# Layer-1 pairs moved from two SBUF buffers into one PSUM bank, and the other banks divided anew

## What is computed

```python
x0 = xk = e                                   # (1024, 39, 16)
for W in (f0, f1, f2):                        # (39*39, 128), (128*39, 128), (128*39, 128)
    z = einsum('bfd,bgd->bfgd', x0, xk).reshape(b, 39 * g, 16)
    cur = einsum('bpd,pm->bmd', z, W)         # (1024, 128, 16)
    outs.append(cur); xk = cur
z = concatenate(outs, axis=1).sum(-1)         # (1024, 384)
h = relu(concatenate([z, dense_ctx]) @ W_top1 + b_top1)
h = relu(h @ W_top2 + b_top2)
y = h @ W_top3                                # (1024, 1)
```

## Time and profile before

| | us |
|---|---|
| median of 3 runs | 1325.23 (1324.9 to 1326.23) |
| the profiled execution | 1326.9, with a span of 1325.1 |
| PE busy in the span | 1274.4 (96%) |
| DVE, POOL, ACT busy | 1157.1 (87%), 1052.0 (79%), 913.7 (69%) |

### The profile page before, as it was taken

The page is one execution under the profiler, slowest core; times in us unless marked ns, Lnnn a source line. Parts: engine busy times, 40 slices in busy tenths (PEclk is TensorE's granted clock), DMA queues, the critical chain, the costliest instruction groups (busy, mean ns, idle before and its releaser), DMA issues. The chain is left out here.

```text
span 1325.1 us, 21626 instructions
## 1 busy us (share of the span) xinstructions
PE 1274.4 (96%) x5983; PEld 1015.7 (77%) x5983; DVE 1157.1 (87%) x3210; ACT 913.7 (69%) x3053; POOL 1052.0 (79%) x743
## 2 busy tenths in 40 slices
PE   3899999999999999999999999999999999999998
PEld 2587777877788777887778877788777877788787
DVE  3599998799988999689996999969998799988983
ACT  2477776677767777577775777757776677767783
POOL 7688888688877888778986888968888688874661
PEclk9799999999999999999999999999999999999999
DMA  5582233332223332213333033331233332223000
GB/s 135 104 206 46 49 62 65 62 62 43 43 52 63 63 65 58 43 34 62 67 64 64 5 64 66 65 61 23 51 62 65 62 58 44 46 54 61 1 3 1
DMA packets 129499, 76.33 MB, mean 58 GB/s; under 512 B 90792, under 2 KB 98201, under 8 KB 129379
## 3 DMA queue, kind: packets, MB, share of 16 engines
q1 hardware_dynamic: 119139, 72.32, 26.8%
q0 software_dynamic: 10240, 2.64, 2.3%
HBM read 68.42 MB, written 3.87 MB: 55 GB/s over the span
## 5 line engine op out<-in xcount | busy, mean ns | idle before, releaser
L397 ACT ACTIVATE parts<-pieces,x_cols 128x128 f32<-128x128 f32 x2560 | 716.0, 376 | 172.3 <-PE pieces L693 156.3
L531 DVE SCALAR_TENSOR_TENSOR parts<-pieces,x_cols,parts 128x128 f32<-128x128 f32 x2432 | 679.9, 341 | 115.5 <-PE pieces L693 89.6
L691 PE MATMUL pieces<-w_hi,cur_hi 128*128 128x512 f32 (+1 forms) x1280 | 548.3, 428 | 18.2 <-DVE parts L531 16.8
L693 PE MATMUL pieces<-w_hi,cur_lo 128*128 128x512 f32 (+1 forms) x1280 | 498.9, 390 | 0.0
L692 PE MATMUL pieces<-w_lo,cur_hi 128*128 128x512 f32 (+1 forms) x1280 | 498.5, 389 | 0.0
L346 POOL TENSOR_TENSOR parts<-parts 128x1024 f32<-128x1024 f32 x127 | 320.1, 2520 | 134.8 <-DVE parts L531 131.4
L337 POOL DMA_INDIRECT emb<-in_table,rows x320 | 345.1, 1078 | 80.9 <-issue 67.4
L691 PEld LDWEIGHTS pieces<-w_hi,cur_hi 128*128 128x128 f32 x1280 | 241.8, 189 | 89.4 <-DVE parts L531 38.4
L693 PEld LDWEIGHTS pieces<-w_hi,cur_lo 128*128 128x128 f32 x1280 | 240.9, 188 | 51.6
L692 PEld LDWEIGHTS pieces<-w_lo,cur_hi 128*128 128x128 f32 x1280 | 242.2, 189 | 47.8
L416 ACT ACTIVATE pairs_hi<-pairs 117x512 fp32r<-117x512 f32 (+1 forms) x224 | 141.9, 634 | 193.8 <-DVE pairs L541 161.9
(11 more groups left out here) (69 smaller groups left out, 594.7 us busy)
## 6 DMA issues: line engine op xcount, KB each, us to landing
partners<-x_wide SPq DMA_DIRECT2D x62, 546.0 KB
partners<-x_wide SPq DMA_DIRECT2D x31, 468.0 KB
x_rep<-x_wide SPq DMA_DIRECT2D x96, 78.0 KB
emb<-in_table,rows POOLq DMA_INDIRECT x320
x_diag<-x_cols SPq DMA_DIRECT2D x256, 10.0 KB
x_wide<-emb SPq DMA_DIRECT2D x32, 80.0 KB
x_wide<-emb SPq DMA_DIRECT2D x32, 32.0 KB
wt<-in_wt SPq DMA_DIRECT2D x1, 1024.0 KB
```

The costliest lines, as they stand in the source:

```text
L397: last = nc.scalar.activation(parts[n % 2][:, 4 * i + r, :], src[:, r * H:(r + 1) * H], ACT.Copy, scale=x_cols[n // 4][:, n % 4, f:f + 1])
L531: nc.vector.scalar_tensor_tensor(acc, src[:, r * H:(r + 1) * H], x_cols[n // 4][:, n % 4, f:f + 1], acc, ALU.mult, ALU.add).then_inc(acc_d ...
L691: nc.tensor.matmul(dst[:, 0:width], hi[:, cols], w1_hi[:, ws], start=True, stop=False)
L693: nc.tensor.matmul(dst[:, 0:width], lo[:, cols], w1_hi[:, ws], start=False, stop=True).then_inc(l2d_ready if q in D_PIECES else l2a_ready, 1)
```

## The change

The eight banks are divided anew.

- `pairs` is one bank of PSUM in place of two buffers of SBUF. `make_pairs` writes it, ACT's high part and DVE's low part read it. With one buffer, `make_pairs` waits for the low part of the round before (it was: of the one two before). The first tile's pairs stay in SBUF (in `partners[0]`), so the load of tile 2's partners gets a wait for the seventh low part.
- `gx_bank` holds both the 320 columns of `make_g` and, behind them, the turned fields (39 rows turned in place of 78). So a turning waits for the copy of the last G, and `make_g` waits for the copy of the last turned fields. The turning is at s = 17 of every tile (it was 14, 20, 30 and 20).
- `cur1_bank` takes, beside the first layer's sum, layer 3 and the tower. They run between two such sums: `layer3` in ten steps of four fields at 39 to 48, its copy at 49; `top1` at 79 to 82, ReLU at 83 and 84; `top2` at 86 and 87, ReLU at 88; `top3` at 119. They wait until the sum before has been taken, and the next `sum_pairs` (s = 10, that is at 50, 90 and, in the next tile but one, 130) waits for `l3_copied`, `h2_copied` and `y_copied`.
- The first four G of a quad, which must follow layer 3, move from steps 38, 42, 52, 62 to 49, 53, 60, 64; there are three `cur2` buffers in place of two.
- The pieces keep five banks.

```diff
-XT_ROWS = 2 * F
-X_STEP = XT_ROWS
+X_AT = 320
...
-S_G = [2, 12, 22, 32]
-S_G_FIRST = [2, 12, 22, 38]
-
-L3_STEP = 3
-S_L3 = range(25, 25 + F // L3_STEP)
-S_L3_COPY = 38
-S_H1 = range(41, 41 + N1 // P)
-S_RELU1 = range(45, 47)
-S_H2 = range(50, 50 + N2 // P)
-S_RELU2 = 52
-S_Y = 55
+S_X = 17
+
+
 G_LAG = 3
+G_STEP = {10 * n + 32: (0, n) for n in range(4, BLOCKS - G_LAG)}
+G_STEP.update({49: (0, 0), 53: (0, 1), 60: (0, 2), 64: (0, 3), 2: (1, 13), 12: (1, 14), 22: (1, 15)})
+
+L3_STEP = 4
+S_L3 = range(39, 39 + (F + L3_STEP - 1) // L3_STEP)
+S_L3_COPY = 49
+S_H1 = range(79, 79 + N1 // P)
+S_RELU1 = range(83, 85)
+S_H2 = range(86, 86 + N2 // P)
+S_RELU2 = 88
+S_Y = 119
 Q_HALVE, Q_FINISH = 7, 8
+CURS = 3
...
-S_X = [14, 20, 30, 20]
...
+def g_made(u, at):
+    late = [s for s, (back, _) in G_STEP.items() if s < at and (back == 0 or u > 0)]
+    return max(0, u * BLOCKS - G_LAG) + len(late)
+
+
+def x_turned(u, at):
+    return min(QUADS * TILES, u * TILES + 1 + len([i for i in range(TILES) if 4 * PIECES * i + S_X <= at]))
...
-        pairs = [sb(f"pairs{i}", [KPART, COLS]) for i in range(2)]
...
-        xbank = bank("xbank")
+        pairs = bank("pairs")
         cur1_bank = bank("cur1_bank")
-        gbank = bank("gbank")
-
-        h_sums = [xbank[:, m * P:(m + 1) * P] for m in range(N1 // P)]
+        gx_bank = bank("gx_bank")
+
+        x_turns = [gx_bank[:, X_AT + j * F:X_AT + (j + 1) * F] for j in range(4)]
+        h_sums = [cur1_bank[:, m * P:(m + 1) * P] for m in range(N1 // P)]
         h1_last = [pieces[m][:, 0:P] for m in range(N1 // P)]
-        h2_last = [pieces[4][:, m * P:(m + 1) * P] for m in range(N2 // P)]
+        h2_last = [pairs[:, m * P:(m + 1) * P] for m in range(N2 // P)]
...
+        first_banks = pieces + [pairs, gx_bank]
+        first_pairs = partners[0]
...
+                if tile == 2:
+                    sp.wait_ge(pairs_lo_ready, PAIRK)
...
+                src = gx_bank[:, X_AT:X_AT + 4 * F].rearrange("p (j f) -> p j f", f=F)
+                nc.scalar.activation(x_cols[i][:, :, 0:F], src, ACT.Copy).then_inc(x_cols_ready, 1)
...
-                nc.scalar.activation(pairs_hi[buf][0:rows, :], pairs[buf][0:rows, :], ACT.Copy
-                                     ).then_inc(pairs_hi_ready, 1)
+                src = first_pairs[0:rows, k, :] if tile == 0 else pairs[0:rows, :]
+                nc.scalar.activation(pairs_hi[buf][0:rows, :], src, ACT.Copy).then_inc(pairs_hi_ready, 1)
...
-                wait(dve, pairs_lo_ready, g - 1)
-                nc.vector.tensor_tensor(pairs[buf][0:rows, :], partners[i % 2][0:rows, k, :], x_rep[i % 2][0:rows, :],
+                dve.wait_ge(pairs_lo_ready, g)
+                nc.vector.tensor_tensor(pairs[0:rows, :], partners[i % 2][0:rows, k, :], x_rep[i % 2][0:rows, :],
...
-                nc.vector.tensor_tensor(pairs_lo[buf][0:rows, :], pairs[buf][0:rows, :],
+                src = first_pairs[0:rows, k, :] if tile == 0 else pairs[0:rows, :]
+                nc.vector.tensor_tensor(pairs_lo[buf][0:rows, :], src,
...
+            def transpose_x(tile, i, gs):
 
                 pe.wait_ge(x_rep_loaded[i % 2], (tile - i % 2) * 8 * REP + 16 * REP)
                 wait(pe, x_cols_ready, tile)
-                if i == 2 and not first:
-                    pe.wait_ge(y_copied, (tile - i) // TILES)
+                wait(pe, g_copied, gs)
                 for j in range(4):
-                    last = nc.tensor.transpose(xbank[:, j * X_STEP:(j + 1) * X_STEP],
-                                               x_rep[i % 2][0:XT_ROWS, j * P:(j + 1) * P], ident[0:XT_ROWS, 0:XT_ROWS])
+                    last = nc.tensor.transpose(x_turns[j], x_rep[i % 2][0:F, j * P:(j + 1) * P], ident[0:F, 0:F])
...
+                if first_banks[k] is gx_bank:
+                    pe.wait_ge(x_cols_ready, 1)
...
+                    if i == 2:
+                        wait(pe, l3_copied, tile // TILES)
+                    if i == 3:
+                        wait(pe, h2_copied, tile // TILES)
+                    if i == TILES:
+                        wait(pe, y_copied, tile // TILES - 1)
...
+            def make_g(u, n, turned=QUADS * TILES):
 
                 g = u * BLOCKS + n
                 pe.wait_ge(cur2_ready, g + 1)
+                pe.wait_ge(x_cols_ready, turned)
...
-                    pe.wait_ge(x_cols_ready, tiles)
-                for f in range(step * L3_STEP, (step + 1) * L3_STEP):
-                    last = nc.tensor.matmul(xbank[:, 0:P], w2[:, f, :], G[:, :, f, :], start=f == 0, stop=f == F - 1)
-                if step == F // L3_STEP - 1:
+                    pe.wait_ge(cur1_lo_ready, tiles)
+                    pe.wait_ge(sum1_ready, tiles)
+                for f in range(step * L3_STEP, min(F, (step + 1) * L3_STEP)):
+                    last = nc.tensor.matmul(cur1_bank[:, 0:P], w2[:, f, :], G[:, :, f, :], start=f == 0, stop=f == F - 1)
+                if step == len(S_L3) - 1:
...
+            def top3(u, tiles=QUADS * TILES):
                 pe.wait_ge(h2_copied, u + 1)
+                pe.wait_ge(cur1_lo_ready, tiles)
+                pe.wait_ge(sum1_ready, tiles)
```

More of the change, by code:

```diff
@@ L127, in cin_kernel @@
         tails = [sb(f"tails{i}", [P, 4, H]) for i in range(2)]
-        cur2 = [sb(f"cur2_{i}", [P, H]) for i in range(2)]
+        cur2 = [sb(f"cur2_{i}", [P, H]) for i in range(CURS)]
         x_diag = [sb(f"x_diag{i}", [P, 4, BLK_B, FX]) for i in range(2)]
@@ L483, in quad @@
                             weigh_piece(u, n, q)
+                        at = 4 * PIECES * i + s
                         if more and s in S_HIGH:
                             take_pairs_high(tile + 1, i + 1, S_HIGH.index(s))
-                        if more and s == S_X[i] + 1:
+                        if more and s == S_X + 1:
                             copy_x_cols(tile + 1, (i + 1) % TILES)
-                        if s - 1 in (S_G_FIRST if i == 0 else S_G):
-                            if n >= G_LAG:
-                                copy_g(u, n - G_LAG)
-                            elif not first:
-                                copy_g(u - 1, BLOCKS + n - G_LAG)
-                        at = 4 * PIECES * i + s
+                        if at - 1 in G_STEP:
+                            back, b = G_STEP[at - 1]
+                            if u >= back:
+                                copy_g(u - back, b)
                         if not first:
@@ L534, in make_pairs @@
             def make_pairs(tile, i, k):
-                g, buf, rows = tile * PAIRK + k, (i * PAIRK + k) % 2, rows_of(k)
+                g, rows = tile * PAIRK + k, rows_of(k)
                 if k == 0:
@@ L548, in make_first_pairs @@
                 dve.wait_ge(first_partners, k + 1)
-                wait(dve, pairs_lo_ready, k - 1)
-                nc.vector.tensor_tensor(pairs[k % 2][0:rows, :], first_banks[k % len(first_banks)][0:rows, :],
-                                        x_rep[0][0:rows, :],
+                nc.vector.tensor_tensor(first_pairs[0:rows, k, :], first_banks[k][0:rows, :], x_rep[0][0:rows, :],
                                         ALU.mult).then_inc(pairs_ready, 1)
@@ L740, in top2 @@
                     last.then_inc(h2_ready, 1)
-            def top3(u):
+            def top3(u, tiles=QUADS * TILES):
                 pe.wait_ge(h2_copied, u + 1)
+                pe.wait_ge(cur1_lo_ready, tiles)
+                pe.wait_ge(sum1_ready, tiles)
                 for k in range(N2 // P):
-                    last = nc.tensor.matmul(xbank[0:1, 0:P], wt3[:, k:k + 1], h2[:, k, :], start=k == 0,
+                    last = nc.tensor.matmul(cur1_bank[0:1, 0:P], wt3[:, k:k + 1], h2[:, k, :], start=k == 0,
                                             stop=k == N2 // P - 1)
@@ L776, in quad @@
                         n, q = 4 * i + s // PIECES, s % PIECES
+                        at = 4 * PIECES * i + s
                         layer2_piece(u, n, q)
-                        if more and s == S_X[i]:
-                            transpose_x(tile + 1, (i + 1) % TILES, first)
+                        if more and s == S_X:
+                            transpose_x(tile + 1, (i + 1) % TILES, g_made(u, at))
                         if more and s in S_SUM:
                             sum_pairs(tile + 1, i + 1, S_SUM.index(s))
-                        if s in (S_G_FIRST if i == 0 else S_G):
-                            if n >= G_LAG:
-                                make_g(u, n - G_LAG)
-                            elif not first:
-                                make_g(u - 1, BLOCKS + n - G_LAG)
-                        at = 4 * PIECES * i + s
+                        if at in G_STEP:
+                            back, b = G_STEP[at]
+                            if u >= back:
+                                make_g(u - back, b, x_turned(u, at))
                         if not first:
@@ L814, in _ @@
             make_g(u, BLOCKS - 1)
-            for step in range(F // L3_STEP):
```

(1 more changed line is left out.)

32 lines of the change are left out of this document (13 added, 19 removed).

## The result

The changed kernel takes 1332.24 us as the median of six runs (1330.91 to 1335.05), the kernel before 1325.66 us in its six (1324.9 to 1327.19). The ratio is 1.0051, with a 95% interval from 1.0038 to 1.0065. So it is slower by 0.5%, where 1315.2 us and faster was forecast, and it lies 1.2 us above the range. Three of the six runs are at 1331 us and three at 1333.4 to 1335.05. The profiled one, 1334.33 us with a span of 1332.5, is of the upper three.

What follows compares the result with a forecast made beforehand. PE's matmuls fill most of each tile; DVE, held up by POOL's adds, makes PE wait. Terms -19.2 + 11.2 - 2 = -10.0 on 1326.9 give 1316.9; the median, 1.7 lower, is 1315.2 us, range 1298 to 1331.

Steps and rivals of the forecast that it cites:

- Low part (L558) should fall to about 683 ns: DVE's 192 wide low parts, reading pairs from PSUM, fall from 949 to about 683 ns, 1.6 us a tile.
- I take 1.2 us of the 2.1 for a light tile: Tiles without layer 3 and tower: PE regains 1.2 of 2.1 us lost to waits; ends 0.3 and 2.0.
- its DVE and POOL meet as in tile 3: Reason for counting tile 0 of quads 1 to 7 among the tiles that gain 1.2 us each.
- a sign of being wrong: The forecast would be wrong if tiles without layer 3 and tower stayed above 36.2 us.
- light tiles: Tiles without layer 3 and tower, 16 after the change: -19.2 us together, between -5 and -32.
- the relief is handed back: Rival, chance 0.10: earlier DVE meets POOL in products instead; tiles without layer 3 and tower gain 0.5 us; 1326 us.
- The new waits in tile 2: PE waits for ReLUs at top2 and the sum_pairs at 90: 2.5 us a quad, net +11.2 us over seven quads.
- The turning at 17 lies five steps ahead of the next G: Turning and G share a bank; the turning at step 17 was listed as costing nothing (three steps ahead in tile 1).
- Turning 39 rows for 78: Halves 124 short PE matmuls, busy 13.9 us in all, weight loads stay: -2 us, between 0 and -5.
- The product writing to PSUM: DVE's product (L541) writes PSUM and keeps two SBUF operands: no difference, ends 0 and +0.1 us.
- The wait for the sum at step 39: DVE finishes 0.1 us before PE needs the sum: no cost, up to 0.3 us a quad if lost.

Runs made afterwards that it cites:

- The table of four: Ratios to the kernel before: pairs in SBUF 1.0071 with the waits in tile 2, 0.9985 with both ReLU steps early; pairs in PSUM 1.0051 and 0.9916.

## Why the prediction was wrong

Its sum was -10.0 us on the profiled execution; +7.4 came. By its steps:

- **"Low part (L558) should fall to about 683 ns"**: right, 679. The PSUM operand does end the block, and the longer PSUM read of the Trainium skill, "VectorE: DVE Perf Modes", section "The TRN2 errata", does not show in it: the low part of the short round, of 78 rows, takes 675 ns from PSUM, where it had 676 from SBUF.
- **"I take 1.2 us of the 2.1 for a light tile"**: this is the step that failed, with the reason given for tile 0, that "its DVE and POOL meet as in tile 3". The runs with the pairs back in SBUF measure the term by itself: the operand is worth 2.6 us of the time in place of 19.2, and 9 us once the two waits are gone. By tile: in tile 0 it wins 0.2 us with the waits (37.79 to 37.58) and 0.1 without (37.79 to 37.66); in tile 3 0.1 and 1.16. Against the kernel before, tile 0 got 0.5 us worse, 7 x 1.7 = 12 us off the forecast, and at 37.6 us it stands above the 36.2 that the prediction had named as a sign of being wrong. Quad 0's three light tiles, which were to win 3.6 us, won nothing (110.03 us before, 110.06 after). Tile 3 won 1.8 us, 3.6 us more than forecast over six quads, and that is partly luck: the pause in tile 2, put in as a pure cost, is enough for it without the operand. The working assumed that a DVE that is earlier brings POOL's add forward and so shortens the block of the first product. It did so in tile 3 (2.44 to 1.63 us). In tile 0 the first product gained 0.3, the second lost 0.85 (1.69 to 2.54) and a third, free before, took 1.68. The rival **the relief is handed back** had the mechanism, and I gave it 0.10. The run with one operand shows what all blocks of products cost once the two waits are gone, 24 us.
- **The new waits in tile 2**: right. 2.5 us a quad was the forecast, 2.47 a quad came off with them. What the prediction didn't ask is what they do to the other term: the pause relieves DVE, so the relief of the low part buys less. It allowed for the pause in tile 2 alone and added up the tiles. The table of four shows that they aren't one.
- **"The turning at 17 lies five steps ahead of the next G"**, costed at nothing: it failed too. I looked at the G behind the turning, not at the one before it, at step 12, whose copy must leave the shared bank and stands on ACT behind the high part of a blocked product. PE waits there 11.7 us in ten places. As a cause it is worth little (the copy's move gave 0.05%), since DVE would be late one piece further on.
- **The clock**: not in the sum. A wait of 2.39 us was followed by the half clock; together they cost 3.6 us in quad 5, some 2.4 of it the clock. That is likely why three runs lie 3 us above the other three: their mean clock is 0.995 against 0.996 to 0.997. Only one of the six was profiled, so this isn't shown for the others.
- **"Turning 39 rows for 78", -2**: a second failed term, of the wrong sign. The four matmuls are busy as long as before (234 ns each, from 230), and the turning holds PE 0.69 us from start to start where it held it 0.46: +0.23 a tile, up to +7 us over 31 tiles. Why is open.
- The product writing to PSUM was costed at nothing: right. Unblocked it takes 0.69 us, from 0.68. The wait for the sum at step 39 (L734 on DVE's L579) came to 1.1 us in five places.

The terms against what they measured, in us: light tiles -19.2, measured -10.8 in tile 3, +3.5 in tile 0 and 0 in quad 0; tile 2 +11.2, measured +11.2; not foreseen: the long wait and the clock in quad 5 +3.6, tile 1 +1.4. These add up to +8.9 against the +7.4 found, as close as single windows, multiplied, come. The dearer turning stands in each of these figures, 0.23 us a tile; it is all of tile 1's.

Still open: why tile 0 settles into long blocks and tile 3 into short ones. The run with one gather moved shows that POOL's phase matters, but I didn't find an order in which both tiles are short.

## What to carry to other kernels

Where two engines hold each other up, freeing one kind of operation does not free the engine: it moves the collision to the next operation that can still collide. Price such a change by the most that all collisions cost (one run that removes them all), and expect little until all of them are gone. Gains and waits that fall on the same late engine don't add: measure them two by two. And when several uses share a bank, look for the copy that must empty it, and at what stands ahead of that copy on its own engine; a swap of two steps there was worth more (1.35%) than the change's whole idea (0.7%).

## What the runs showed of the hardware

- A DVE operation with two SBUF operands that waited for POOL was not served between two back-to-back POOL adds: 3.20 us, through adds of 1.29 and 1.27 us, and 2.75 us through two of 1.30 on the kernel before. Cutting POOL's add in two made the block of that product longer (2.53 to 3.20 us), that of the first product shorter (2.42 to 1.57), and the mean stayed (1039 and 1043 ns, wide form). The Trainium skill, "SBUF — State Buffer", section "Who interferes with whom", says that a DVE instruction with two SBUF inputs contends with a GpSimd one that reads SBUF, and one with at most one doesn't; the trace agrees, with 684 ns for the product and 679 for the low part with one operand, 1043 and 949 with two.
- One idle stretch of PE of 2.39 us, in a kernel whose PE is 95% busy, was followed by some 7 us at 1.2 GHz, and one of 2.0 us in the run with G's copy first by some 3 us. Of the waits of 2.51 us in the split run some were followed by 3 us of it and some by 7. But the wait of 2.38 us in the run with the early ReLU was followed by none, and so were the waits of 1.1 us: tile 0 of quad 3 has a clock of 1.00. How long PE waits does not by itself say whether the clock falls.
- Of the operations of 512 columns here, an operand read from PSUM was not slower than one from SBUF: on 78 rows the low part takes 675 ns from PSUM and 676 from SBUF. The product of 78 rows takes 687 ns into PSUM and 678 into SBUF. ACT's copy of the pairs takes 602 ns from PSUM, where it had 634 from SBUF.
- Four turning matmuls are busy as long with 39 rows as with 78. Their price to PE is another: 0.46 us from the matmul ahead to the one behind where their first weight load ran beside the matmul ahead, 0.69 where it came 0.32 us behind that one's start.
